# Gram-Schmidt on Gram matrices, f32 scores in four row groups, and a new order of two halves, in a four-layer kernel on one core

## The reference

```python
def gram_schmidt(X):
    for i in range(r):
        q = Q[:, i] / (norm(Q[:, i]) + EPS)
        Q = Q.at[:, i].set(q)
        Q = Q.at[:, i + 1:].add(-outer(q, q @ Q[:, i + 1:]))
basis = gram_schmidt(U) @ gram_schmidt(V).T
feats = (h @ basis) @ basis.T[:, :32]
out = h + strength * (feats @ resp_w.T + resp_b + safety_bias)
```

## Time and profile before

| what | us |
|---|---|
| median of 3 runs | 157.54 |
| lowest, highest | 156.97, 163.27 |
| span of the profiled execution (first to last instruction) | 155.5 |
| own time of the profiled execution | not listed apart from the three runs; the median is 2.0 above the span |
| mean granted TensorE clock | 0.799 |

### The profile page before, as it was taken

How to read it: one execution, slowest core, us unless ns; L and a number is a source line. 1 busy time by engine, 2 the same in 40 slices (tenths; PEclk the granted TensorE clock), 3 DMA queues, 4 the chain that set the end, 5 groups by cost and what they waited for, 6 DMA issues and landing times.

```text
span 155.5 us, 3723 instructions
## 1 busy us (share of the span) xinstructions
PE 131.8 (85%) x1448; PEld 77.0 (50%) x1448; DVE 82.7 (53%) x306; ACT 56.2 (36%) x130; POOL 78.5 (51%) x168
## 2 busy tenths in 40 slices
PE   6799999998867497499999397999979987898970
PEld 2235754376424132355644175576344933667960
DVE  0510244943688755866765935377564374427413
ACT  8992051123113005820556700232128426311210
POOL 0345257533689947867633725449555974300000
PEclk9999996599999659955558955555899999999555
DMA  4894000000000000000000000000000000000102
GB/s 151 271 361 189 0 4 0 2 0 0 2 0 4 0 0 0 6 0 6 0 4 0 4 4 4 0 0 4 4 0 0 0 4 0 4 0 0 67 0 67
DMA packets 2252, 4.53 MB, mean 29 GB/s; under 512 B 411, under 2 KB 923, under 8 KB 2235
## 3 DMA queue, kind: packets, MB, share of 16 engines
q1 hardware_dynamic: 2235, 4.30, 8.1%
HBM read 3.77 MB, written 0.52 MB: 28 GB/s over the span
## 4 chain that ended last, share of the span: by engine, by line
PE 59%; POOL 16%; DVE 9%; issue 5%; ACT 4%; DMA 2%; SPq 2%; POOLq 0%; DVEq 0%
PE G L286 7%; PE S L311 5%; POOL gsr L891 4%; POOL gsn L885 4%; PE B L331 4%; PE S L276 3%; PE B L371 3%; PE S L453 2%; PE S L444 2%; PE S L446 2%; PE S L445 2%; PE B L347 2%; PE B L345 2%; POOL gsne L888 2%; PE S L435 2%
## 5 line engine op out<-in xcount | busy, mean ns | idle before, releaser
L885 POOL TENSOR_TENSOR gsn<-gsn,half_pos 64x1 f32<-64x1 f32 x32 | 18.7, 584 | 37.3 <-ACT gsq L683 37.3
L683 ACT ACTIVATE gsq<-G 64x128 f32<-64x128 f32 x32 | 8.6, 270 | 55.6 <-PE G L286 55.5
L1041 DVE SCALAR_TENSOR_TENSOR gs_pack<-G,gsf,gs_pack 64x128 f32<-64x128 f32 x32 | 10.9, 341 | 25.5 <-POOL gsf L895 25.3
L286 PE MATMUL G<-gs_pack 32*32 32x128 f32 x128 | 15.6, 327 | 8.5 <-DVE gs_pack L1041 7.3
L1035 DVE CUSTOM_DVE_ANT_0 gsjunk<-gs_pack,G 64x128 f32<-64x128 f32 x32 | 10.8, 336 | 21.1 <-ACT gsq L683 21.1
L891 POOL TENSOR_TENSOR gsr<-gsne,minus_two 64x1 f32<-64x1 f32 x32 | 18.3, 572 | 2.7
L286 PEld LDWEIGHTS G<-gs_pack 32*32 32x32 f32 x128 | 5.0, 115 | 24.6 <-DVE gs_pack L1041 18.3
L444 PE MATMUL S<-kh,qbh 32*128 32x32 f16 x128 | 11.4, 185 | 2.5 <-DVE qbl L1162 2.5
L444 PEld LDWEIGHTS S<-kh,qbh 32*128 32x128 f16 x128 | 10.5, 99 | 2.9 <-DVE qbl L1162 2.8
L445 PEld LDWEIGHTS S<-kl,qbh 32*128 32x128 f16 x128 | 10.7, 101 | 1.7 <-issue 1.7
L276 PE MATMUL S<-filler 128*128 128x512 bf16 x26 | 10.1, 546 | 1.2 <-DVE filler L1078 1.2
(11 more groups left out here) (153 smaller groups left out, 269.7 us busy)
## 6 DMA issues: line engine op xcount, KB each, us to landing
rows<-in_rows SPq DMA_DIRECT2D x1, 576.0 KB, 6.8
xT<-in_xT SPq DMA_DIRECT2D x1, 512.0 KB, 5.3
w<-in_w SPq DMA_DIRECT2D x1, 512.0 KB, 7.6
w<-in_w0b SPq DMA_DIRECT2D x1, 320.0 KB, 3.0
w<-in_w SPq DMA_DIRECT2D x1, 288.0 KB, 5.8
w<-in_w0a SPq DMA_DIRECT2D x1, 256.0 KB, 2.7
xF<-in_xFa SPq DMA_DIRECT2D x1, 256.0 KB, 2.9
xF<-in_xFb SPq DMA_DIRECT2D x1, 256.0 KB, 4.4
```

Source lines behind the costliest of these rows:

```text
L286: j = mm(G[half, 0:P], view(ident, k * R + i, [(0, R)], k * R, R), uv[half, :], start=True, stop=True)
L885: nc.gpsimd.tensor_tensor(gsn[:, i:i + 1], gsn2[:, i:i + 1], half_pos[:], ALU.pow)\
L1041: v.scalar_tensor_tensor(uv[:], G[0:2 * R, 0:P], gsf[:, i:i + 1], uv[:], ALU.mult, ALU.add).then_inc(s["gs_col"], 1)
```

## The change

**Gram-Schmidt.** TensorE makes the two 32x32 Gram matrices once (`gs_gram`). VectorE then keeps, for the 64 rows of both matrices, a tile `gsw` of 64 columns: the Gram matrix of what is left in columns 0 to 31, and the triangular matrix of the transformation in columns 32 to 63. A step shuffles row i to all rows of its half (`gs_row`), GpSimd takes the root of the diagonal element, and seven VectorE operations update the tile. ScalarE and TensorE have no part in a step. There are 31 steps (0 to 30). At the end the triangle is scaled and turned, and one product per matrix (`gs_basis`) applies it to U and V; `gs_vectors` copies the results to uo and vo. `gs(n)` runs n steps in a row. The reciprocal moves from GpSimd's power to VectorE.

**Scores.** One f32 product per sequence and row group in place of three f16 ones; the sequence is the outer loop and the four row groups take turns. The high and low splits go from ScalarE, VectorE and GpSimd. One call makes all four banks.

**Order.** The first half's L1 moves between the parts of the second half's L0 on TensorE. L1_up and the values now go to bank G, which Gram-Schmidt no longer holds. Most keep_warm calls go. The identity is a DMA of its own (64 KB) behind the gs load, which becomes 128 KB instead of 160 KB.

```diff
+            def gs_gram():
+                pe.wait_ge(ld["gs"], 16)
                 for k in range(2):
                     half = slice(k * R, (k + 1) * R)
+                    j = mm(G[half, 0:R], gs_cols[:, half], gs_cols[:, half], start=True, stop=True)
+            def gs_basis():
+                pe.wait_ge(s["gs_turned"], 1)
...
+                    j = mm(G[half, 0:P], gstT[half, :], uvT[half, :],
+            def scores(t, *free):
...
+                for r in range(Q):
+                    mm(S_[r][:], maskl[rows_, :], view(maskr, 0, [(0, HB), (1, S)], r * A, A),
                 pe.wait_ge(s["q_split"], t + 1)
-                pe.wait_ge(s["k_split"], t + 1)
+                pe.wait_ge(s["k_ready"], t + 1)
                 for b in range(HB):
...
-                    mm(o, qs, kh[t][rows_, sl], start=False, stop=False, skip_group_check=True)
-                    mm(o, qs, kl[t][rows_, sl], start=False, stop=False, skip_group_check=True)
-                    i = mm(o, qsl, kh[t][rows_, sl], start=False, stop=(b == HB - 1),
+                    for r in range(Q):
+                        rows_ = slice(r * A, (r + 1) * A)
+                        i = mm(S_[r][:, sl], qb[t][rows_, b * P:(b + 1) * P], k32[t][rows_, sl],
+                               start=False, stop=(b == HB - 1), skip_group_check=True)
```

VectorE's new functions:

```diff
+            def gs_row(i):
+                v.stream_shuffle(gsb[i % 2][:], gsw[:, i:i + R + 1], [i] * R)\
+            def gs_step(i):
+                dve.wait_ge(s["gs_root"], i + 1)
+                v.tensor_tensor(gsu[:, one], gss[:, one], gs_eps[:, one], ALU.add)\
+                v.reciprocal(gsr[:, one], gsu[:, one]).then_inc(s["gs_rec"], 1)
+                v.scalar_tensor_tensor(gsf[:, one], row[:, 0:1], gsr[:, one], gsr[:, one],
+                v.scalar_tensor_tensor(gsc[:, one], gsw[:, one], gsr[:, one], gsr[:, one],
+                v.scalar_tensor_tensor(gse[:, one], gsf[:, one], 2.0, gsc[:, one],
+                v.scalar_tensor_tensor(gsw[:, R:R + 1 + i], row[:, R - i:R + 1], gsc[:, one],
+                v.scalar_tensor_tensor(gsw[:, i + 1:R], row[:, 1:R - i], gse[:, one],
+                if i < R - 2:
+                    gs_row(i + 1)
             def split_q(t):
-                v.tensor_tensor(ql[t][:], q32[t][:], qh[t][:], ALU.subtract)\
                 for h in range(Q):
+                    i = v.tensor_scalar(view(qb[t], h * S, [(P, HB), (1, S)]), qs_(q32[t]),
```

More of the change, by code:

```diff
@@ L190, in build @@
         G = ctx.enter_context(nc.psum_tensor("G", [P, 512], F32))
[L193 removed]
+        ld = {k: sem("ld_" + k) for k in ("ids", "col", "bf", "w0", "x0", "w0b", "gs", "ident", "expert",
                                           "x1", "xT", "w1", "rows", "w2", "w3")}
@@ L227, in stepper, with gs @@
             state = [0]
-            def gs():
-                one(state[0])
-                state[0] += 1
+            def gs(n):
+                for _ in range(n):
+                    one(state[0])
+                    state[0] += 1
             return gs
@@ L246, in _ @@
             load(gs_pack[:], "gs", "gs")
+            load(ident[:], "ident", "ident")
             load(exp_pack[:], "expert", "expert")
@@ L341, in L0_third @@
                 pe.wait_ge(s["h_ready"], 4 * t + 4)
-                for c in range(Q):
+                for c in range(c0, c1):
                     tok = slice(c * P, (c + 1) * P)
@@ L544, in _ @@
             L0_first(0, 3)
-            gs()
             L0_second(0)
-            L0_third(0)
-            gs()
+            pick_experts()
+            L0_third(0, 0, Q)
             L0_third_sr(0)
@@ L576, in _ @@
             L1_up(1, ("y1_sum", 1))
[L577 to L578 removed]
             to_F("h", 0, ("aF_ready", 2))
[L580 removed]
             queries(0, ("z_ready", 2))
[L582 to L591 removed]
+            keys(0, ("y0_sum", 2))
+            values(0, ("y1_sum", 2))
+            keep_warm(S_[3], 3, ("h_ready", 8))
+            scores(0, ("hid_ready", 2), ("hid2_ready", 2), ("h_ready", 8))
+            to_F("h", 1, ("hF_ready", 1))
+            queries(1, ("q_ready", 1))
+            keys(1, ("k_ready", 1))
             subtract(0, 0)
[L593 to L595 removed]
             subtract(0, 1)
@@ L1337, in _ @@
+            maxima(1, 3)
+            gs(2)
+            sum_x1(0)
+            stats(3, 0)
+            gs(1)
+            apply(3, 0)
             turn(1, 0)
-            gs_dot()
-            maxima(1, 2)
-            sum_x1(0)
-            gs_update()
             turn(1, 1)
-            maxima(1, 3)
-            gs_dot()
-            stats(3, 0)
             turn(1, 2)
             turn(1, 3)
-            gs_update()
-            gs_dot()
-            apply(3, 0)
-            gs_update()
+            gs(2)
```

483 lines of the change are left out of this document (161 added, 322 removed).

## The result

The changed kernel takes 171.08 us (median of 4 runs, 169.97 to 174.23) beside 159.51 us for the kernel before on the same chip: a ratio of 1.0855 [1.0745, 1.0966]. The forecast was 162.0 us with a range of 149 to 170. It is slower, as the likelier side of the forecast had it, but 9.1 us beyond the number (span 169.1 where 160.0 was worked out) and 1 us beyond the range.

A forecast was written before the change was run, and what follows sets the result against it. VectorE's in-order stream was taken as the bound: scores done at 72.3 us, then 26.55 + 17.5 + 18.45 to the last step at 134.8, vectors at 140.0, 20.0 remaining: span 160.0, 2.0 more for 162.0 us; range 149 to 170.

The forecast's parts named there:

- the likelier side of the forecast: Whole kernel: slower by over 2%, given 0.47, against 0.30 for within 2% and 0.23 for faster.
- the chain mostly VectorE: Sign of being right: the chain that ended last would be mostly VectorE, with GpSimd's roots.
- From there VectorE alone sets the pace: From the first half's maxima (scores done at 72.3 us), VectorE's operations were summed to the last step at 134.8.
- 10.35 us from the maxima to the split: VectorE, first half: maxima 2.6, apply 1.1, step 1.35, four transposes 2.75, step 1.35, split 1.2.
- a wait only at the contexts: Two of four contexts stand behind the second half's scores on TensorE, so VectorE waits 2.55 us.
- The signs of being wrong: Lone step under 1.8 us, scores at 0.07 or 0.3 us per product, last six steps starting long before 123, clock 1.00 through scores.
- clock rival: TensorE at 1.2 GHz after idling: two ff_in, basis, ff_out and matrices cost some 6 us more, 168 us; chance 0.12.
- faster rival: VectorE links of 0.12 us give back 8.6 us, scores at the high clock 4.5 more: about 149 us; chance 0.23.
- point of turning: Step price of about 1.1/1.8 us (beside other work/back to back) from which the sign of the change turns.
- no-overlap rival: Row groups don't overlap f32 loads: each half's scores 17 to 30 us instead of 6.4, 180 us or more; chance 0.08.

The follow-up runs named there:

- a4: Changed kernel with filler products in four places where TensorE waits: 167.1 us, ratio 1.0545.
- a1: Changed kernel with the first half's subtracts ahead of the second half's transposes, queries and keys on TensorE, exponentials earlier on ScalarE: 168.81 us, ratio 1.0654.
- a2: Changed kernel with the row group as outer loop of the scores, so row groups don't take turns: 203.14 us, ratio 1.2853.
- b4: Changed kernel with subtracts earlier, first half's gate before the last six steps, fillers, and second half's L0 end first: 159.17 us, ratio 1.0097.
- d1: c1 with GpSimd's skip_sum moved from beside the apply to beside the transposes: 147.87 us, ratio 0.9364.
- c2: c1 with feed-forward, pools and gates of both halves beside the last steps: 160.23 us, ratio 1.0106.
- c1: b4 with first half's contexts ahead of second half's scores, rstd ahead of skip_sum, and some steps moved earlier: 156.25 us, ratio 0.9723.

## Why the forecast came out as it did

**What held.** VectorE's in-order stream has become a large part of the bound (32% of the chain, 100.8 us busy), though "the chain mostly VectorE" didn't come true: TensorE has 44%. A lone step costs 2.15 us (2.05 forecast), a hidden one 1.4 (1.35). The experts' placing ended at 20.1 (19.9), apply(0,0) began at 27.1 (26.6), the first L1 sum at 36.4 (it was to end at 37.0, and ended at 37.1), the second half's L0 apply ended at 52.1 (51.9), the maxima began at 72.5 (72.3), the tail took 20.5 us (20.0).

**The step that failed** is "From there VectorE alone sets the pace", with its 10.35 us from the maxima to the split and a wait only at the contexts. Between maxima and turns lie TensorE's subtracts and ScalarE's exponentials, and in the new stream the subtracts stand behind to_F(h,1), queries(1) and keys(1), where the kernel before had them ahead of queries(1). The sum treats VectorE's next instruction as ready when the one before ends; it didn't follow TensorE's order at this point, although the stream was printed. It is worth 5.6 us in place, 2.5 of them by the low clock of that stretch (a4), and 2.1 to 3.2 at the end (a1). That the late turn explains 5.4 of the 9.1 us holds for the marks, not for what its removal gives.

**Sizes that were off.** The steps: 2.15 for 2.05, by the links with per-partition scalars (1.32 for 1.20 from the sum to the shuffle) and not by the root. From the last step to the vectors: 7.4 us for a forecast of 5.2, since transposes and two ff_in ran at the low clock (1.08 and 3.38 for 0.45 and 1.75). The scores: one half at 0.057 and one at 0.10, for 0.10 on both (the bounds were 0.066 at the high clock and 0.116 at the low one). The 2.7 us gained on the first half didn't reach VectorE: the values ended at 66.7 for 64.9 (0.9 us late already at the L1 sum, then queries, keys and values in 5.0 for 4.0, the first two at the low clock), and the scores ended at 71.3, but VectorE came to the maxima only at 72.5, from its own statistics and a step.

**The signs of being wrong.** Scores at 0.07 us and a clock of 1.00 through them were to show a faster kernel. Both came in the first half, and the kernel was slower, for the reason just given.

**The clock rival** was given 0.12, at 168 us, the nearest of all to the 171.1 measured. Its mechanism did act, at the turn (2.5 us) and ahead of the basis (2.2), and fillers bring back 3.7 to 4.9 us; but where it looked for its 6 us, in ff_out and the matrices, the clock was high (1.16 us an ff_out, as before).

**The faster rival's** point of turning was a step of 1.1/1.8; with 1.4/2.15 it is out. The no-overlap rival is out (a2).

**The loss as a whole.** Without steps the changed kernel is 10 to 12 us longer than the one before without steps, and the new steps cost 2 to 4.5 us more than the old. Most of the loss can be had back by order and fillers: b4 gives 12 us. With the same instructions in another order, some 90 fillers more and later starts of skip_sum (d1), the kernel is 6.4% faster than the one before and 14% faster than as changed (0.9364/1.0855 = 0.863). Two things stay open: no run sets the scores back to three f16 products, and the kernel before was not given the same reordering, so the 6.4% don't say what the new Gram-Schmidt is worth by itself.

## What to carry to other kernels

When a chain moves onto the engine that carries the main path, every queue must be followed anew at each hand-over: ask for each wait what stands ahead of its producer, on the producer's engine. An operation moved into an idle stretch is free only if its producer isn't late there (c2, 5.45 us) and no GpSimd operation beside it holds it up (c1, 3.70 us for 1.10). What looks like a wait for an order can in part be a low clock; a filler at the place tells the two apart, as in a4, where it took 2.5 of the turn's 5.6 us.

## What the hardware showed that was not expected

**GpSimd stretches VectorE, and only some of its operations.** In the changed kernel, step 5 beside a0(0), VectorE's timeline:

```profile
28.48 1.13 DVE L930 SCALAR_TENSOR_TENSOR gsf<-gsb,gsr 64x1 f32<-64x1 f32 x1
29.54 0.20 DVE L932 SCALAR_TENSOR_TENSOR gsc<-gsw,gsr 64x1 f32<-64x1 f32 x1
29.85 1.10 DVE L936 SCALAR_TENSOR_TENSOR gse<-gsf,gsc 64x1 f32<-64x1 f32 x1
```

and GpSimd's beside them:

```profile
28.33 1.27 POOL L826 TENSOR_TENSOR tmp<-n,rows 128x512 f32<-128x512 f32 x1 [0.36 <-DVE n L971]
29.68 1.26 POOL L829 TENSOR_TENSOR a0T<-tmp,b0u 128x512 f32<-128x512 f32 x1
```

VectorE's first and third take 0.21 and 0.15 us elsewhere. Here they end when GpSimd's operation beside them ends: 29.61 and 29.60, 30.95 and 30.94. So each is held until that operation ends, not slowed by a factor. The step beside a0(1) and a1_bo(0), from 52.03, has three operations held in the same way. In this kernel both steps lay in slack and cost the path little; in c1 and c2 the same neighbour made an apply of four operations 3.70 us instead of 1.10, and d1 took it away. Transposes (d1) and statistics (at 122.20 in the changed kernel, beside skip_sum at 122.24) did not stretch. The Trainium skill (GPSIMD Engine Reference, Key points) says that GpSimd shares its SBUF interfaces with VectorE and contends with instructions that have two SBUF inputs or run in a two-port mode; the runs agree, with these numbers, and the apply has one tensor input from SBUF, so by that rule it would be one of the latter, which no run here shows by itself.

**The clock of an early stretch scatters for the same stream**: 0.86 and 0.72 at 20 to 36 us in two profiled runs with equal instructions up to there, with 5.4 us between them at the first L1 sum. The other traces with the same stream up to there have that sum at 38.3 to 41.7 us.

**f32 products in row groups in turn** cost 0.057 us each at the high clock and 0.10 at a mean clock of 0.56, against 0.39 at 0.51 out of turn (a2): about a quarter, with four row groups.
